# Layer 2: the high part of the turned x is read from its SBUF copy, and one copy alone releases the PSUM bank

## The chip, the cores and the metric

The kernel runs on one core of a Trainium2 chip, in one launch. The metric is the device time of that launch in microseconds (us); lower is better. Engines: PE (TensorE, matmuls and transposes, results in PSUM), ACT (ScalarE), DVE (VectorE), POOL (GpSimd, which works on SBUF alone here) and SP (SyncE, which issues transfers). Each runs its own list in order and waits for the others by semaphores.

## The reference, cut to what matters

Four graph layers on x of 16 batches x 512 nodes x 128 features follow one another: an Euler scheme, a two-layer GCN with batch norms, a masked self-attention and a graph attention. After each: `x = _layernorm(x + layer(x))`. The change lies in the third, "layer 2":

```python
def _L2_gnn_ref(h, W, adj):            # h: (16, 512, 128), W: (128, 384), 4 heads of 32
    qkv = h @ W
    q, k, v = split(qkv)
    mask = jnp.where(adj == 0, -jnp.inf, 0.0)
    scores = jnp.einsum('bhid,bhjd->bhij', q, k) / np.sqrt(HEAD_DIM) + mask
    attn = jax.nn.softmax(scores, axis=-1)
    out = jnp.einsum('bhij,bhjd->bhid', attn, v)
    return out
x = _layernorm(x + _L2_gnn_ref(x, L2_gnn_W, adj), axis=-1)
```

## The kernel before, in words

Layer 2 takes the 16 batches one after another, as a software pipeline. A step s works on several batches at once, each at another stage; each engine has a written list of items with the number of steps by which the item's batch lies behind s (`"x:2"`: the turning of x for batch s-2). The lists are `PE_ORDER`, `ACT_ORDER`, `DVE_ORDER`, `POOL_ORDER` and `SP_ORDER`, repeated for every step (L92 is the loop's end). There is no scheduler: what stands in the list runs in that order, each item after its own waits. Steps count from 0; the first has only the first items, a full step has all.

PE's list for one step, with the items that the prediction uses:

```
v:4 k:3 t2:5 D0:6 D1:6 s0:3 x:2 n:4 t3:5 d:6 T:0 s1:3 o:6 t0:4 V0:5 V1:5 s2:3 q:2 t1:4 V2:5 V3:5 s3:3
```

- T (L1822) turns layer 1's result of batch s; DVE's R (L1732) then adds the residual, into `Xb`.
- x (L1827) turns the normed x of batch s-2 into a PSUM bank. ACT copies it out twice: xc (L1670) as full float32, `xT`, and xh (L1666) cast to fp32r, `xT_hi`. POOL's xl (L1619) subtracts the two, `xT_lo`. The product q takes `xT_hi` and `xT_lo` (L59 to L61).
- s0 to s3 (L1852) are scores of a quarter of the rows, four heads each. DVE's u0 to u3 (L1755) take their masked row maxima.
- t0 to t3 (L1868, then the mask with L1872) are the transposed scores of one head, into the two wide PSUM tiles of 1024 columns. ACT exponentiates each with two activations (E0 to E7, L1693). t0 also needs the first two tiles of u1, whose banks it takes, and POOL adds halves of the exponentials (S0 to S3, L1624) for the denominators.
- V0 to V3 (L1890), D0 and D1 (L1880), d (L1901) and o (L1896) form the output and its denominators and turn them back. DVE's c1 (L1761), c2 (L1768) and r (L1775) divide and add the residual; r alone of these reads two SBUF operands. ACT's y (L174, out `X`) applies the layer norm from step 7 on.

ACT's list: `E0 E1 Y qh E2 E3 f vc kh N E4 E5 e xc nr E6 E7 y xh`. So xc stands before the last two exponentials of the step and xh behind them and behind y. ACT's qh (L1674) waits for the transfers of q and k that SP issued for the batch two before (L1593).

Two PSUM banks, called the ring, serve the short-lived products. One of them holds, in PE's order, v, x, T, o and q (and D). `wait_for_bank` makes PE wait before each of these for the item that emptied the bank; `released` names the semaphore. For the bank that holds x this is `x_hi`, the end of xh. The next user is T; in steps 16 and 17, which have no T any more, it is o. Step 18 has no x in that bank ahead of it.

Of the kernel before, what the change touches and what calls it, by code (L numbers as in the profile page):

```python
# [41 lines left out]
def after(b, per, k=None):  # L42

    return (b + CREDIT) * per + (per if k is None else k)


def hold(eng, gate):


    eng.sem_inc(gate, 1)  # L50


def flat(ap):
    return ap.rearrange("p a b -> p (a b)")
# [44 lines left out]
def tile_of(X, b, t):  # L99
    return X[:, bass.ds(b, 1), t].rearrange("p a d -> p (a d)")  # L100
# [986 lines left out]
def staged(text):  # L1087

    return [(word.split(":")[0], int(word.split(":")[1])) for word in text.split()]
# [374 lines left out]
def layers2_3(nc, m, bank, wide, out):  # L1464
# [4 lines left out]
    with ExitStack() as own:  # L1469
        def sb(name, shape, dt=F32):  # L1470
            return own.enter_context(nc.sbuf_tensor(name, shape, dt))

        def sem(name):
            return own.enter_context(nc.semaphore(name))
# [3 lines left out]
        xT = [sb(f"xT{k}", [P, N]) for k in range(2)]  # L1478
        xTr = [sb(f"xT_{h}", [P, N], F32R) for h in ("hi", "lo")]
# [23 lines left out]
        x_ps = sem("x_turned"); x_hi = sem("xT_high"); x_c = sem("xT_out"); x_lo = sem("xT_low")  # L1503
# [26 lines left out]
        ring = {name: bank[6 + k] for name, k in staged("T:1 x:1 k:0 v:1 q:1 n:0 D0:1 V0:0 d:0 o:1")}  # L1530
# [3 lines left out]

        def released(name, b):

            return {"x": (x_hi, after(b, 1)), "q": (q_lo, after(b, 1)), "k": (k_lo, after(b, 1)),
                    "v": (v_c, after(b, 1)), "n": (n_row, after(b, 1)), "D0": (d_c, after(b, 1)),
                    "V0": (o_c, after(b, 1)), "d": (rcp, after(b, 1)), "o": (o_n, after(b, 1)),
                    "T": (res1, after(b, 1))}[name]  # L1540
# [8 lines left out]
        def run(eng, items, act_on, last=None):  # L1549

            depth = 1 + max(back for _, back in items)

            def step(s, par, alive, nth):
                for name, back in items:
                    if alive[back]:
                        act_on(name, s - back, (par + back) % 2, s, alive)

            pairs(eng, B, depth, step, last=last)
# [13 lines left out]
        @block.sync  # L1572
        def _(sp):
            for h in range(H):
                sp.sem_inc(row_in[h], CREDIT * 16)
                sp.sem_inc(stacked[h], CREDIT * STACKED)

            def transfer(name, b, bp, s, alive):
                h = int(name[2])
                sp.wait_ge(t_ps, after(b - 1, H, h + 1))  # L1580
                hold(sp, gate)
                if name[0] == "d":
                    sp.wait_ge(n_row, after(b, 1))
                    hold(sp, gate)
                    sp.dma_start(q_st[3 * HD:3 * HD + 1, h].bitcast(F32).rearrange("a (t p) -> a t p", p=P),
                                 neg_row[h * NT:h * NT + NT].bitcast(F32)).then_inc(row_in[h], 16)
                else:
                    sp.wait_ge(q_lo, after(b, 1))
                    hold(sp, gate)
                    sp.wait_ge(k_lo, after(b, 1))  # L1590
                    hold(sp, gate)
                    for g, (q, k) in enumerate(((Q_HI, K_HI), (Q_HI, K_LO), (Q_LO, K_HI))):
                        sp.dma_start(qk_st[g * HD:(g + 1) * HD, :, h].bitcast(F32),  # L1593
                                     qkT[bp][h * HD:(h + 1) * HD, q:k + 1:k - q].bitcast(F32)).then_inc(stacked[h], 16)

            run(sp, SP_ORDER, transfer)
            third.sync(sp)
# [41 lines left out]
        @block.scalar  # L1639
        def _(act):  # L1640
            third.act_credits(act)
            for s in (bn, x_hi, x_c, q_hi, k_hi, v_c, n_row, o_c, d_c):
                act.sem_inc(s, CREDIT)
            act.sem_inc(t_exp, CREDIT * EXPS)
            for n in (norm1, norm):
                n.credit_apply(act)

            def projections_free(b):
                for h in range(H):
                    act.wait_ge(stacked[h], after(b - 2, STACKED))  # L1650
                act.wait_ge(s_ps, after(b - 2, TILES))

            def work(name, b, bp, s, alive):
                if name == "N":
                    act.wait_ge(b_ps, after(b - 1, 1))
                    hold(act, gate)
                    act.activation(on[:], m.O[:, bass.ds(b, 1)].rearrange("p a n -> p (a n)"), ACT.Identity,
                                   scale=m.aff2[:, 0, 0:1], bias=m.aff2[:, 1, 0:1]).then_inc(bn, 1)
                elif name == "Y":
                    norm1.apply_act(act, b + CREDIT, bp, Xf[bp], lambda k: Xf[bp][:, k])  # L1660
                elif name == "y":
                    norm.apply_act(act, b + CREDIT, bp, r, lambda k: tile_of(m.X, b, k))
                elif name == "xh":
                    act.wait_ge(x_ps, after(b, 1))
                    act.wait_ge(k_ps, after(b - 1, 1))
                    act.copy(xTr[0][:], ring["x"][:]).then_inc(x_hi, 1)  # L1666
                elif name == "xc":
                    act.wait_ge(x_ps, after(b, 1))
                    act.wait_ge(v_ps, after(b - 2, 1))
                    act.copy(xT[bp][:], ring["x"][:]).then_inc(x_c, 1)  # L1670
                elif name == "qh":
                    projections_free(b)
                    act.wait_ge(q_ps, after(b, 1))
                    act.copy(qkT[bp][:, Q_HI], ring["q"][:]).then_inc(q_hi, 1)  # L1674
                elif name == "kh":
                    projections_free(b)
                    act.wait_ge(k_ps, after(b, 1))
                    act.copy(qkT[bp][:, K_HI], ring["k"][:]).then_inc(k_hi, 1)
                elif name == "vc":
                    act.wait_ge(v_ps, after(b, 1))  # L1680
                    act.wait_ge(av, after(b - 2, NT))
                    act.copy(flat(v[bp][:]), ring["v"][:]).then_inc(v_c, 1)
                elif name[0] == "E":
                    k = int(name[1])
                    h, half = divmod(k, 2)
                    act.wait_ge(t_ps, after(b, H, h + 1))
                    if k == 0:
                        act.wait_ge(av, after(b - 2, NT))
                        act.wait_ge(h_sum, after(b - 2, H))
                    if k == 4:  # L1690
                        act.wait_ge(av, after(b - 1, NT))
                        act.wait_ge(h_sum, after(b - 1, H))
                    act.activation(flat(prob[bp][h][:, 2 * half:2 * half + 2]), wide[half][:], ACT.Exp,  # L1693
                                   scale=SCALE).then_inc(t_exp, 1)
                elif name == "nr":
                    act.wait_ge(n_ps, after(b, 1))
                    for h in range(H):
                        act.wait_ge(row_in[h], after(b - 1, 16))
                    act.activation(neg_row[:], ring["n"][0:TILES, 0:P], ACT.Copy, scale=-1.0).then_inc(n_row, 1)
                elif name == "e":  # L1700
                    act.wait_ge(dn, after(b, 2))
                    act.wait_ge(d_ps, after(b - 1, 1))
                    act.copy(denT[:], ring["D0"][:]).then_inc(d_c, 1)
                elif name == "f":
                    act.wait_ge(av, after(b, NT))
                    act.wait_ge(o_ps, after(b - 1, 1))
                    act.copy(oT[:], ring["V0"][:]).then_inc(o_c, 1)

            run(act, ACT_ORDER, work, last=18)
            item = third.act_items(act)  # L1710
            tail("E0.14 E1.14 E2.14 E3.14 f.13 vc.15 E4.14 E5.14 e.13 nr.15 E6.14 E7.14 3XR.0 3X.0 y.12 E0.15 E1.15 3W0.0 "
                 "E2.15 E3.15 f.14 3W1.0 E4.15 E5.15 e.14 E6.15 E7.15 3G.0 3L0.0 3L1.0 y.13 3XR.1 3L2.0 3L3.0 3X.1 f.15 e.15 "
                 "3E0.0 3W0.1 3W1.1 y.14 3E1.0 3XR.2 3G.1 3L0.1 3L1.1 3X.2 3L2.1 y.15", ACT_ORDER, work, item)
            pairs(act, B, 4, third.in_order(item, third.act_order), last=B, first=3)
            third.act_last(act, item)
# [232 lines left out]
```

## Time and profile before

| | us |
|---|---|
| median of 3 runs | 1008.46 |
| the runs | 1007.96, 1008.46, 1016.79 |
| the profiled execution's own time | 1007.55 |
| its span | 1005.6 |
| PE busy in the span | 886.4 (88%) |
| DVE busy | 643.3 (64%) |
| ACT busy | 505.2 (50%) |
| POOL busy | 362.7 (36%) |

Layer 2 runs from about 457 us to about 860 us of the span; its last steps overlap with layer 3. "m" below is the start of the mask matmuls of t3 (L1872) in a step: a point that every step from 5 on has, shortly before T. The end of a stretch is the start of s2, behind T, s1, o, t0, V0 and V1. In the step whose m is at 603.82, T is at 608.42 and s2 at 614.92. The mean granted clock of TensorE over the span is 0.956 of full speed.

A row of the timeline reads: start, duration, engine, line, operation, output<-input, count, and in brackets the idle time of the engine before it with what ended it.

### The profile page before, as it was taken

Reading aid. Unit: us, or ns where it says so; the run is one execution under the profiler, and the core shown is the slowest. Engines: PE = TensorE matmul, PEld = TensorE weight load, DVE = VectorE, ACT = ScalarE, POOL = GpSimd, SP = SyncE. Lnnn points to the kernel's source line nnn. Section 1 sums busy time; section 2 is a strip of 40 time slices with the busy share of each in tenths; the row PEclk is TensorE's granted clock in tenths of the full one; section 3 lists DMA queues with packets and bytes.
Section 4 is the critical chain, followed back from the end, with each engine's and each line's share of the span. In section 5 each row is a group of like instructions: output and inputs, shape, how many; then the busy total and the mean of one; then the engine's idle time right before and its main releaser. Section 6 shows DMA issues by size and latency. Waiting matters only on the chain. (4 is left out here: it accounts for less than half of the span.)

```text
span 1005.6 us, 20699 instructions
## 1 busy us (share of the span) xinstructions
PE 886.4 (88%) x6039; PEld 632.9 (63%) x6039; DVE 643.3 (64%) x1960; ACT 505.2 (50%) x903; POOL 362.7 (36%) x417
## 2 busy tenths in 40 slices
PE   6999999999998899795688888777888898899996
PEld 5799999999997878432334444333444344577775
DVE  4755554555455776474866666666666573799997
ACT  4322211212112255574356666666666657888884
POOL 4011021011111020003345666655666547355554
PEclk9999999999999899898789899999999899999999
DMA  8000000000001000000332222233233331011111
GB/s 235 21 11 12 22 12 12 21 10 21 10 0 21 22 0 0 1 0 18 70 73 65 64 64 63 63 72 69 63 67 75 78 82 34 2 32 31 31 31 42
DMA packets 34242, 40.74 MB, mean 41 GB/s; under 512 B 6672, under 2 KB 17552, under 8 KB 34192
## 3 DMA queue, kind: packets, MB, share of 16 engines
q1 hardware_dynamic: 32816, 39.87, 16.6%
q8 instruction: 24, 0.39, 0.2%
q10 hardware_dynamic: 1376, 0.27, 0.1%
q14 instruction: 26, 0.21, 0.1%
HBM read 6.43 MB, written 4.19 MB: 11 GB/s over the span
## 5 line engine op out<-in xcount | busy, mean ns | idle before, releaser
L1693 ACT ACTIVATE prob<-wide 128x1024 f32<-128x1024 f32 x128 | 124.1, 1021 | 102.1 <-PE wide L1872 102.1
L1624 POOL TENSOR_TENSOR half_sum<-prob 128x1024 f32<-128x1024 f32 x64 | 150.1, 2368 | 42.3 <-PE bank L1880 41.2
L431 ACT CAST yT<-wide 128x512 fp32r<-128x512 f32 x48 | 28.1, 589 | 206.2 <-PE wide L827 156.8
L1755 DVE CUSTOM_DVE_ANT_0 junk<-wide,mask_ij 128x512 bf16<-128x512 f32 x128 | 82.8, 684 | 64.1 <-PE bank L1852 63.7
L1868 PE MATMUL wide<-qk_st 128*128 128x512 f32 x256 | 92.1, 473 | 2.8 <-ACT prob L1693 1.3
L1755 DVE CUSTOM_DVE_ANT_0 junk<-bank,mask_ij 128x512 bf16<-128x512 f32 x128 | 83.0, 685 | 0.0
L531 POOL TENSOR_TENSOR Xr<-Xf,Xr 128x512 fp32r<-128x512 f32 x16 | 20.4, 1290 | 168.2 <-ACT Xr L426 168.0
L1439 PEld LDWEIGHTS bank<-Wh,pr 128*128 128x128 f32 x512 | 65.2, 191 | 15.9 <-ACT pr L1292 7.0
L1439 PE MATMUL bank<-Wh,pr 128*128 128x129 f32 x512 | 68.5, 278 | 6.7 <-ACT pr L1292 6.0
L59 PE MATMUL bank<-z,L3T_hi 128*128 128x256 f32 x256 | 73.3, 286 | 0.4 <-DVE zf L646 0.4
L60 PE MATMUL bank<-z,L3T_hi 128*128 128x256 f32 x256 | 73.0, 285 | 0.0
L61 PE MATMUL bank<-z,L3T_lo 128*128 128x256 f32 x256 | 72.9, 285 | 0.0
L1868 PEld LDWEIGHTS wide<-qk_st 128*128 128x128 f32 x256 | 52.6, 218 | 27.4 <-DVE mx L1755 15.2
L153 POOL TENSOR_SCALAR n_rstd<-n_aggr 128x4 f32<-128x4 f32 x31 | 6.6, 212 | 166.7 <-DVE n_aggr L146 161.4
L1890 PE MATMUL bank<-prob,v 128*32 128x512 f32 x512 | 65.3, 630 | 1.2 <-ACT prob L1693 1.2
L623 DVE TENSOR_TENSOR yT<-wide,yT 128x512 fp32r<-128x512 f32 x48 | 33.0, 688 | 35.0 <-ACT yT L431 34.8
L1822 PE MATMUL bank<-ident,on 128*128 128x128 f32 x64 | 11.7, 312 | 47.4 <-ACT xT_hi L1666 39.8
L59 PEld LDWEIGHTS bank<-z,L3T_hi 128*128 128x128 f32 x256 | 49.5, 193 | 1.8 <-issue 0.9
L1732 DVE TENSOR_TENSOR Xb<-bank,X 128x512 f32<-128x512 f32 x16 | 11.1, 691 | 61.1 <-PE bank L1822 58.2
L60 PEld LDWEIGHTS bank<-z,L3T_hi 128*128 128x128 f32 x256 | 49.5, 193 | 0.3
L61 PEld LDWEIGHTS bank<-z,L3T_lo 128*128 128x128 f32 x256 | 49.5, 193 | 0.0
L646 DVE TENSOR_TENSOR zf<-bank,G 128x256 f32<-128x256 f32 x64 | 26.9, 420 | 31.2 <-PE bank L61 29.5
(304 smaller groups left out, 2400.8 us busy)
## 6 DMA issues: line engine op xcount, KB each, us to landing
qk_st<-qkT SPq DMA_DIRECT2D x192, 128.0 KB, 2.4
out_dram<-rc SPq DMA_DIRECT2D x15, 256.0 KB, 2.3
Xf<-X SPq DMA_DIRECT2D x14, 256.0 KB, 2.3
A<-in_adj_dram SPq DMA_DIRECT2D x4, 256.0 KB, 4.7
qk_st<-neg_row SPq DMA_DIRECT2D x64, 2.0 KB
Xf<-in_x_dram SPq DMA_DIRECT2D x2, 256.0 KB, 6.7
mask_q<-mask_ji SPq DMA_DIRECT2D x16, 32.0 KB, 1.8
w<-in_L_gnn_W_dram SPq DMA_DIRECT2D x2, 128.0 KB, 2.3
```

Of the source, the lines that this page charges most:

```text
L59: pe.matmul(out, stat[0], mov[0], start=start, stop=False)
L60: pe.matmul(out, stat[0], mov[1], start=False, stop=False)
L61: return pe.matmul(out, stat[1], mov[0], start=False, stop=stop)
L431: act.copy(yT[bb][i][0][:], psum_y[i][:]).then_inc(y_hi, 1)
L623: dve.tensor_tensor(yT[bb][i][1][:], psum_y[i][:], yT[bb][i][0][:].bitcast(F32), ALU.subtract).then_inc(y_lo, 1)
L646: dve.tensor_tensor(zf[:, t], psum_h[k % 2][:, 0:GB * D], G[1 - par][:, 1 if k < NT else 0, t], ALU.add).then_inc(h_sb, 1)
L1439: last = pe.matmul(out_bank[h][:, t * (D + 2):t * (D + 2) + D + 1], pr[par][:, j, k * P:k * P + P], Wh[par][:, j, 0:D + 1], start=(j == 0) ...
L1624: pool.tensor_tensor(flat(half_sum[h][:]), flat(prob[bp][h][:, 0:2]), flat(prob[bp][h][:, 2:4]), ALU.add).then_inc(h_sum, 1)
L1693: act.activation(flat(prob[bp][h][:, 2 * half:2 * half + 2]), wide[half][:], ACT.Exp, scale=SCALE).then_inc(t_exp, 1)
L1755: dve.tensor_tensor_reduce(out=junk[h % 2][:], in0=ROWS[h][:], in1=m.mask_ij[:, i], scale=1.0, scalar=3.0 * MASKED, op0=ALU.add, op1=ALU.m ...
L1868: pe.matmul(bank[j][:], k_st[:, k, j * P:j * P + P], q_st[:, k], start=True, stop=True)
L1890: last = pe.matmul(ring["V0"][c, :], v[bp][:, k, c], prob[bp][h][:, k], start=(k == 0), stop=(k == NT - 1), skip_group_check=True)
```

## The change

The cast xh no longer reads the PSUM bank but `xT`, the float32 copy that xc has put into SBUF, and so it waits for xc (`x_c`) instead of for PE (`x_ps`). The bank counts as free when xc is done. The semaphore of xh stays as it is for those that read `xT_hi`. No instruction is added, dropped or moved on any engine: the lists are the same, and only the wait of T (steps 2 to 15) and of o (steps 16 and 17) names another semaphore.

```diff
--- before.py
+++ after.py
@@ -1534,7 +1534,7 @@
 
         def released(name, b):
 
-            return {"x": (x_hi, after(b, 1)), "q": (q_lo, after(b, 1)), "k": (k_lo, after(b, 1)),
+            return {"x": (x_c, after(b, 1)), "q": (q_lo, after(b, 1)), "k": (k_lo, after(b, 1)),
                     "v": (v_c, after(b, 1)), "n": (n_row, after(b, 1)), "D0": (d_c, after(b, 1)),
                     "V0": (o_c, after(b, 1)), "d": (rcp, after(b, 1)), "o": (o_n, after(b, 1)),
                     "T": (res1, after(b, 1))}[name]
@@ -1661,9 +1661,9 @@
                 elif name == "y":
                     norm.apply_act(act, b + CREDIT, bp, r, lambda k: tile_of(m.X, b, k))
                 elif name == "xh":
-                    act.wait_ge(x_ps, after(b, 1))
+                    act.wait_ge(x_c, after(b, 1))
                     act.wait_ge(k_ps, after(b - 1, 1))
-                    act.copy(xTr[0][:], ring["x"][:]).then_inc(x_hi, 1)
+                    act.copy(xTr[0][:], xT[bp][:]).then_inc(x_hi, 1)
                 elif name == "xc":
                     act.wait_ge(x_ps, after(b, 1))
                     act.wait_ge(v_ps, after(b - 2, 1))
```

## Rows read from the trace of the kernel before

**Rows 1.** Who waited for the cast xh (L1666), over the whole span.

```profile
  PE bank L1822: 39.8, 14
  PE bank L1896: 4.6, 2
```

**Rows 2.** Timeline of PE in the step with m at 603.82: d and T.

```profile
604.18 0.66 PE L1901 MATMUL bank<-ident,denT 128*128 128x128 f32 x4
608.42 0.65 PE L1822 MATMUL bank<-ident,on 128*128 128x128 f32 x4 [3.59 <-ACT xT_hi L1666]
612.70 0.43 PE L1872 MATMUL wide<-mask_q,identb 32*32 32x512 bf16 x16
```

**Rows 3.** Timeline of ACT in the same step: xc, E6 and E7, y, xh, E0 and E1, qh.

```profile
602.43 0.59 ACT L1670 COPY xT<-bank 128x512 f32<-128x512 f32 x1 [0.82 <-PE bank L1827]
...
604.36 1.94 ACT L1693 ACTIVATE prob<-wide 128x1024 f32<-128x1024 f32 x2 [1.19 <-PE wide L1872]
606.19 1.64 ACT L174 ACTIVATE X<-rb,n_shift,n_rstd 128x128 f32 x4
607.73 0.57 ACT L1666 CAST xT_hi<-bank 128x512 fp32r<-128x512 f32 x1
613.39 1.94 ACT L1693 ACTIVATE prob<-wide 128x1024 f32<-128x1024 f32 x2 [5.10 <-PE wide L1872]
...
616.76 0.57 ACT L1674 CAST qkT<-bank 128x512 fp32r<-128x512 f32 x1
```

**Rows 4.** Stretches from m to s2, steps 5, 6, 7, 9, 15, 16, 17, 18; granted clock behind POOL.

```profile
509.03:519.72 10.69, 7.84 (x61) 2.36 (x60) 5.04 (x21) 5.81 (x9) 7.34 (x6) 0.71 0.51 109
532.58:542.47 9.89, 7.33 (x70) 3.59 (x69) 5.72 (x23) 4.19 (x5) 8.73 (x7) 0.83 0.40 88
555.08:566.74 11.66, 7.88 (x69) 4.02 (x68) 5.77 (x23) 5.43 (x9) 9.04 (x8) 0.71 0.33 72
603.82:614.92 11.10, 7.21 (x69) 3.73 (x68) 5.72 (x23) 5.46 (x9) 8.22 (x6) 0.85 0.34 74
747.21:758.29 11.08, 7.19 (x69) 3.73 (x68) 5.72 (x23) 5.60 (x9) 8.47 (x6) 0.85 0.34 75
770.92:780.70 9.78, 6.77 (x65) 2.66 (x64) 4.22 (x14) 6.40 (x11) 7.65 (x5) 0.83 0.47 101
793.33:804.22 10.89, 7.88 (x66) 3.42 (x65) 4.22 (x14) 5.87 (x9) 8.35 (x5) 0.69 0.46 98
816.83:823.24 6.41, 5.61 (x66) 2.42 (x65) 4.13 (x14) 5.14 (x8) 6.41 (x4) 1.00 0.49 107
```

**Rows 5.** Timeline of DVE in the step with m at 603.82: R, u1's second tile, r.

```profile
609.36 0.69 DVE L1732 TENSOR_TENSOR Xb<-bank,X 128x512 f32<-128x512 f32 x1 [4.81 <-PE bank L1822]
...
610.69 0.69 DVE L1755 CUSTOM_DVE_ANT_0 junk<-wide,mask_ij 128x512 bf16<-128x512 f32 x1
...
618.09 0.69 DVE L1775 TENSOR_TENSOR rb<-rb,X 128x512 f32<-128x512 f32 x1
```

**Rows 6.** Timeline of PE and DVE in step 18: s1, and u1's second tile.

```profile
818.54 0.49 PE L1852 MATMUL wide<-qkT 32*128 32x512 f32 x2 [0.69 <-ACT prob L1693]
...
819.84 0.69 DVE L1755 CUSTOM_DVE_ANT_0 junk<-wide,mask_ij 128x512 bf16<-128x512 f32 x1
```

**Rows 7.** A group of ACT by form: a cast of this size from SBUF, in layer 0 (busy, mean ns).

```profile
L426 ACT CAST Xr<-Xf 128x512 fp32r<-128x512 f32 x14 | 8.0, 620 | 0.0
```

**Rows 8.** Timelines of POOL and DVE: S2 and S3 in step 9; S2 and S3, and r, of step 19.

```profile
609.60 4.70 POOL L1624 TENSOR_TENSOR half_sum<-prob 128x1024 f32<-128x1024 f32 x2
837.60 4.73 POOL L1624 TENSOR_TENSOR half_sum<-prob 128x1024 f32<-128x1024 f32 x2
840.18 2.70 DVE L1775 TENSOR_TENSOR rb<-rb,X 128x512 f32<-128x512 f32 x1 [0.18 <-DVE rb L1768]
```

**Rows 9.** SP's issue of the last transfers that qh waits for; time to landing, 590 to 640 us.

```profile
608.78 1.98 SPq L1593 DMA_DIRECT2D qk_st<-qkT  x3
...
DMA to landing us min/median/max: 2.3/2.4/2.5
```

## The prediction, written before the change was run

> **What bounds the kernel now.** I read three views, in this order. First, who waited for the instruction that the change touches: PE stood idle 39.8 us before T in 14 steps, and 4.6 us before o in two more, until xh ended [rows 1]. That is 44.4 us of real PE idle time on the engine that is busiest. Second, the timeline of one full step, to see whether anything else would have held T: d, the item ahead of it, ends at 604.18 + 0.66 = 604.84, T starts at 608.42 [rows 2]. ACT had finished xc at 602.43 + 0.59 = 603.02, before d was even through. But xh stands behind E6, E7 and y and starts only at 607.73 [rows 3]. The bank is held by ACT's order, not by work on the bank. Third, the stretches from m to the start of s2, step by step [rows 4]: steps that wait take 9.78 to 11.66 us, and step 18, which has no x before it in the bank, takes 6.41. It is a control inside the same trace: nearly the same items (no T, no q behind it), no wait for xh, and the whole of it at the full granted clock, 1.00. The waiting steps show means of 0.69 to 0.85: of its two levels, 1.2 and 2.4 GHz, the clock was at the lower one for a good part of what follows the idle time. The reader should see that the wait costs more than its own length.
>
> **The new length of a full step.** Times are counted from m. T can start when d is through: 604.84 - 603.82 = 1.02. R follows T's start by 609.36 - 608.42 = 0.94, and the second tile of u1 follows R by 610.69 - 609.36 = 1.33 [rows 2, 5]; so that tile starts at 3.29. In step 18 it is 823.24 - 819.84 = 3.40 from there to s2 [rows 4, 6], at full clock. Sum: 6.69. Does s1 come in time for it? s1 takes the banks that E6 reads, and in step 18 it starts 818.54 - 816.83 = 1.71 behind m [rows 4, 6]. T's work ends at about the same time, and u1's first tile is only reached at about 2.7. So PE's idle time shrinks to about a tenth of a microsecond, and DVE's chain T, R, u1 is what sets t0.
>
> **The sum over the steps.** Steps 7 to 15 take 11.66, 11.34, 11.10, 11.18, 11.07, 11.17, 11.09, 11.18 and 11.08 us (the first, the third and the last are in [rows 4]), together 100.9. Nine times 6.69 is 60.2, so 40.7 is gained. Step 6 (9.89, without y) gains 3.2. Step 5 (10.69) has neither d nor y; T then comes early and s1 is what u1 waits for, as in step 18: 10.69 - 6.41 = 4.3. Steps 16 and 17 have no T, o waits in its place: 9.78 - 6.41 = 3.4 and 10.89 - 6.41 = 4.5 [rows 4]. Together 56.1.
>
> The first three waits of the 14 lie in steps 2 to 4 and make 39.8 less nine of 3.59 less two of 2.58 and 2.07, which is 2.8. There xh follows xc almost at once, and DVE, still with other tiles, often is not ready for R. Bounds are 0 and 2.8; I take 1.0.
>
> **What the edit costs.** xh reads SBUF instead of PSUM. Its row has 0.57, a cast of the same size from SBUF has 0.620 [rows 3, 7]: 0.05 more, 16 times. In front of it is nothing new to wait for, since xc is long done. It ends at 608.30 + 0.05, 4.53 behind m. The next on ACT is E0, which starts 0.69 behind t0's mask matmuls [rows 2, 3]; those lie 614.92 - 612.70 = 2.22 ahead of s2, so E0 is due at 6.69 - 2.22 + 0.69 = 5.16. The cover is 0.6 us, where it was 5.1 before. I cost the longer cast at nothing; if this cover is gone, all steps pay what xh is late. The Trainium skill, "VectorE: DVE Perf Modes", section on the TRN2 errata, speaks against the edit: it gives ScalarE 52 cycles more from SBUF than from PSUM, an estimate of 43 ns at its 1.2 GHz, and by that the sum stays the same; the trace's difference of 0.05 agrees.
>
> **What is late next.** POOL does not move, for xl, S2 and S3 hang on xh, which keeps its place against m. S3 ends at 609.60 + 4.70 = 614.30, 10.5 behind m [rows 8]. DVE's r does move: it follows s2 by 618.09 - 614.92 = 3.17 [rows 4, 5], so it comes at 9.86 instead of 14.27, into the time of S3. In the trace this pair met once: r started at 840.18, while POOL's additions ran until 842.33, and took 2.70 us until 842.88 instead of 0.69 [rows 5, 8]. So r will wait for S3 and end at 10.53 + 0.55 = 11.08, 0.53 late; in steps 16 and 17, where it comes at 9.58, 0.81 late. DVE's statistics and u3 stand behind it, and t2 waits for u3. The loss is between nothing and 9 x 0.53 + 2 x 0.81 = 6.4 us; v and t2 have some play of their own, so I take 3.0. The Trainium skill, "SBUF — State Buffer", section "SBUF: two separate sides", has a rule for it: a VectorE instruction with two SBUF inputs and a GpSimd one that reads SBUF exclude each other for a whole instruction. By it r is blocked as reckoned here; were r not held, the sum would be 3.0 better. The trace agrees with the rule, by the 2.70.
>
> **The sum.** 56.1 + 1.0 - 3.0 = 54.1. Against the profiled execution's own 1007.55 that is 953.5. The median of the runs lies 0.9 above it, so I predict 954.
>
> **The rivals.**
> - *Only the waits go, the clock does not come back* (967). The wait is 44.4 us; if other gaps keep the clock at its lower level as now, 44.4 - 3.0 = 41.4 is gained. For it: the clock takes some time to return after an idle stretch. Against it: step 18, with 0.69 idle ahead of s1, shows 1.00 throughout [rows 4, 6]. Chance 0.12.
> - *Another wait takes part of the place* (970 to 990). t0 comes 4.4 us earlier and needs its head's row from SP, E0's cover is 0.6, r runs into S3. Each us lost in every full step costs 11 or so; with 1.5 to 3 lost it is 971 to 988. For it: three margins of a microsecond or less in one step. Against it: step 18 has the same order of n, row and t0 without a wait. Chance 0.16.
> - *The transfers collide, and it gets slower.* The early t0 releases the next batch's first set of transfers while the last set for this one, issued from 608.78 to 610.76 [rows 9], is still moving. qh waits for that set. It started at 616.76, 12.94 behind m [rows 3]; it is wanted about 4.4 earlier, near 8.5, and the set lands at most 2.5 behind its last issue, at 9.4 at the latest. DVE takes ql only behind r, at 11.0, so qh may be some 2 late for nothing. Each further us costs one per step. Break-even with the 4.4 gained is a landing 6 to 7 us late, where 2.3 to 2.5 is measured in all; at 8 us late it would be about 1007.5 + 11 x 1.5 = 1024. Against it: the range of the landing is narrow even where the sets follow closely. Chance 0.03.
> - *Nothing happens* (1007). T also waits for ACT's N and for d's place; if one of these ended at the same time as xh, the wait would keep its length. Against it: d ends 3.6 us earlier, and T starts 0.12 behind xh in the step [rows 2, 3]. Chance 0.03.
>
> **How the numbers follow.** The forecast has 0.66; its own range is 949 to 961, from the bounds of the r term (0 and 6.4), of the first steps (0 and 2.8) and two or three microseconds of drift. The full range, 948 to 973, adds the clock rival and the lower end of the partial one. A change within 1% (about 10 us) is no change for this kernel's measurement. Faster by over 1%: 0.66 + 0.12 + 0.16 = 0.94; within: 0.03; slower: 0.03.
>
> **What would show each step.** In the new trace PE's idle time before T and o until xh is gone, T starts within 0.1 of d's end, and the granted clock is 1.00 from m to s2. That stretch is 6.5 to 7.0 in steps 7 to 15, and the distance from m to m falls from 23.9 ((747.21 - 603.82) / 6, [rows 4]) to about 19.7. xh takes 0.62. r takes 1.1 to 1.3 instead of 0.69 in these steps and POOL's S2 and S3 stay at 4.7. ACT's idle time before E0 is near 0.6. Wrong would be: a wait of PE before t0 or q of over half a microsecond (the row, the transfers or xl), a clock under 0.9 in the stretch, or r as short as now.

## The result, and the profile after

| | before | changed |
|---|---|---|
| median, run in turn on one chip | 1008.21 (1007.51 to 1016.79, 4 runs) | 959.13 (955.08, 958.99, 959.27) |
| profiled execution's own time | 1007.55 | 959.27 |
| its span | 1005.6 | 957.2 |
| mean granted clock | 0.956 | 0.969 |

The ratio is 0.9486 [0.9426, 0.9545]: 49 us faster, where 54 were forecast. A fourth run of the changed kernel, 1242.74 at a mean granted clock of 0.65, was a disturbed one and is left out of the ratio.

First, who waited for xh. This is the answer for its line in the changed kernel: durations (ns, min/median/max), the first and last start, and then who waited (us, times).

```profile
L1666 ACT CAST xT_hi<-xT x16: 601/610/622, 468.3 to 752.9; 128x512 fp32r<-128x512 f32 x16
...
  POOL xT_lo L1619: 45.8, 15
```

The two lines of PE in [rows 1], 39.8 and 4.6 us, are gone. Only POOL's subtraction is left, which needs the value and not the bank. The cast takes 0.61 instead of 0.57.

Now one full step, with m at 591.66, against [rows 2]. The timeline of PE:

```profile
591.66 0.43 PE L1872 MATMUL wide<-mask_q,identb 32*32 32x512 bf16 x16
592.03 0.66 PE L1901 MATMUL bank<-ident,denT 128*128 128x128 f32 x4
592.52 0.60 PE L1822 MATMUL bank<-ident,on 128*128 128x128 f32 x4
593.29 0.50 PE L1852 MATMUL wide<-qkT 32*128 32x512 f32 x2 [0.17 <-ACT prob L1693]
...
594.14 0.66 PE L1896 MATMUL bank<-ident,oT 128*128 128x128 f32 x4 [0.35 <-DVE Xb L1732]
594.56 1.42 PE L1868 MATMUL wide<-qk_st 128*128 128x512 f32 x4
595.90 0.43 PE L1872 MATMUL wide<-mask_q,identb 32*32 32x512 bf16 x16
...
598.12 0.50 PE L1852 MATMUL wide<-qkT 32*128 32x512 f32 x2
```

T (L1822) follows d (L1901) with no idle time. It starts 0.86 behind m, not 4.60. What idle time the timeline shows in the stretch is 0.17 before s1 and 0.35 before o, which waits for R's reading of the bank. R and the second tile of u1 on DVE, against [rows 5]:

```profile
593.40 0.69 DVE L1732 TENSOR_TENSOR Xb<-bank,X 128x512 f32<-128x512 f32 x1 [1.00 <-PE bank L1822]
...
594.73 0.69 DVE L1755 CUSTOM_DVE_ANT_0 junk<-wide,mask_ij 128x512 bf16<-128x512 f32 x1
```

The tile ends at 595.42, and the weight load of t0's last matmul, which has waited 0.4 for DVE's row maxima, comes at 595.5. From the tile's start to s2 it is 3.39.

The timeline of ACT in the same step, against [rows 3]:

```profile
590.27 0.59 ACT L1670 COPY xT<-bank 128x512 f32<-128x512 f32 x1 [0.82 <-PE bank L1827]
...
592.21 1.94 ACT L1693 ACTIVATE prob<-wide 128x1024 f32<-128x1024 f32 x2 [1.19 <-PE wide L1872]
594.04 1.64 ACT L174 ACTIVATE X<-rb,n_shift,n_rstd 128x128 f32 x4
595.58 0.61 ACT L1666 CAST xT_hi<-xT 128x512 fp32r<-128x512 f32 x1
596.60 1.94 ACT L1693 ACTIVATE prob<-wide 128x1024 f32<-128x1024 f32 x2 [0.41 <-PE wide L1872]
...
600.57 0.59 ACT L1674 CAST qkT<-bank 128x512 fp32r<-128x512 f32 x1 [0.51 <-DMA qk_st<-qkT]
```

xh stands 3.92 behind m, as before (607.73 - 603.82 = 3.91): ACT's work has not moved, PE's has. E0 comes 0.41 behind xh, where it came 5.10 behind it. And qh now waits 0.51 for its transfers, where it waited for nothing.

The stretches, for m to s2 of steps 5, 6, 7, 9, 15, 16, 17 and 18, as in [rows 4]. Behind the start and end stand the length, the busy time (and count) of PE, PEld, DVE, ACT and POOL, the granted clock, the DMA share and GB/s:

```profile
513.99:520.40 6.41, 5.20 (x61) 2.00 (x60) 5.13 (x21) 4.11 (x5) 3.34 (x2) 1.00 0.36 77
533.02:539.38 6.36, 5.94 (x69) 2.80 (x68) 5.32 (x23) 4.12 (x5) 5.73 (x4) 1.00 0.33 72
551.99:558.35 6.36, 5.94 (x70) 2.80 (x69) 5.31 (x23) 5.50 (x9) 4.19 (x4) 1.00 0.31 65
591.66:598.12 6.46, 5.94 (x69) 2.80 (x68) 5.32 (x23) 5.50 (x9) 3.78 (x3) 1.00 0.32 69
710.06:716.51 6.45, 5.93 (x69) 2.80 (x69) 5.31 (x23) 5.65 (x9) 4.01 (x3) 1.00 0.29 62
729.54:735.95 6.41, 5.61 (x65) 2.42 (x65) 4.12 (x14) 5.65 (x9) 4.23 (x4) 1.00 0.34 73
749.00:755.41 6.41, 5.60 (x66) 2.42 (x66) 4.14 (x14) 5.65 (x9) 4.26 (x4) 1.00 0.30 65
768.48:774.89 6.41, 5.61 (x65) 2.42 (x65) 4.12 (x14) 5.14 (x8) 6.41 (x4) 1.00 0.49 106
```

All steps now look like step 18, the control, which itself has not changed (6.41). PE's busy time in them falls too, from 7.21 to 5.94 in step 9 for the same matmuls, since the granted clock is 1.00 where it was 0.85.

Then what got worse. The timelines of DVE and POOL in the same step, against [rows 5, 8]:

```profile
597.50 4.73 POOL L1624 TENSOR_TENSOR half_sum<-prob 128x1024 f32<-128x1024 f32 x2
...
601.28 1.50 DVE L1775 TENSOR_TENSOR rb<-rb,X 128x512 f32<-128x512 f32 x1
602.32 0.52 POOL L162 TENSOR_SCALAR n_rstd<-n_aggr 128x4 f32<-128x4 f32 x1
602.71 0.68 DVE L1739 TENSOR_TENSOR qkT<-bank,qkT 128x512 fp32r<-128x512 f32 x1
```

r is issued in the middle of S3 and takes 1.50 instead of 0.69; it ends 602.78 - 602.23 = 0.55 behind POOL's addition. It is no single case. This is r's own line in the changed kernel, over all batches; the median was 686 before:

```profile
L1775 DVE TENSOR_TENSOR rb<-rb,X x16: 687/1452/2681, 542.5 to 818.8; 128x512 f32<-128x512 f32 x16
```

The whole account, from the profiled executions, with two points that both have (m of step 5 and m of step 18):

| | before | changed | difference |
|---|---|---|---|
| up to m of step 5 | 509.03 | 513.99 | +4.96 |
| the 13 stretches m to s2, steps 5 to 17 | 142.12 | 83.93 | -58.2 |
| the 13 stretches s2 to the next m | 165.68 | 170.56 | +4.9 |
| from m of step 18 to the end of the span | 188.8 | 188.7 | 0 |

### The profile page after: what moved, and what is told of

The parts are those of the page before. It is cut to its first block and busy times, and to the rows that moved or that the text cites. A ratio compares the mean times of both kernels' runs of the same rounds, so it can differ in the third digit from the quotient of the medians.

```text
span 957.2 us, 20699 instructions
## 1 busy us (share of the span) xinstructions
PE 878.5 (92%) x6039; PEld 626.5 (65%) x6039; DVE 651.8 (68%) x1960; ACT 506.8 (53%) x903; POOL 366.2 (38%) x417
## 5 line engine op out<-in xcount | busy, mean ns | idle before, releaser
L1868 PE MATMUL wide<-qk_st 128*128 128x512 f32 x256 | 88.1, 440 | 3.8 <-ACT prob L1693 1.7
L59 PE MATMUL bank<-z,L3T_hi 128*128 128x256 f32 x256 | 74.2, 290 | 0.0
L1868 PEld LDWEIGHTS wide<-qk_st 128*128 128x128 f32 x256 | 46.3, 192 | 35.4 <-DVE mx L1755 24.6
L1890 PE MATMUL bank<-prob,v 128*32 128x512 f32 x512 | 61.6, 598 | 1.2 <-ACT prob L1693 1.2
L59 PEld LDWEIGHTS bank<-z,L3T_hi 128*128 128x128 f32 x256 | 50.4, 197 | 1.2 <-issue 0.4
L1852 PEld LDWEIGHTS wide<-qkT 32*128 32x128 f32 x128 | 12.4, 187 | 55.0 <-ACT prob L1693 29.2
L1328 DVE SCALAR_TENSOR_TENSOR pr<-bank,Wh,rl 128x512 f32<-128x512 f32 x64 | 45.0, 741 | 1.2 <-PE bank L1451 1.1
```

What stands on the lines that cost most here:

```text
L59: pe.matmul(out, stat[0], mov[0], start=start, stop=False)
L1328: dve.scalar_tensor_tensor(out=pr[par][:, k], in0=bank[4 + k % 2][:], scalar=Wh[par][:, k, S2_SLOPE:S2_SLOPE + 1], in1=rl[par][:, k], op0= ...
L1868: pe.matmul(bank[j][:], k_st[:, k, j * P:j * P + P], q_st[:, k], start=True, stop=True)
L1890: last = pe.matmul(ring["V0"][c, :], v[bp][:, k, c], prob[bp][h][:, k], start=(k == 0), stop=(k == NT - 1), skip_group_check=True)
```

## The experiments

Nine kernels ran. Ratios are to the kernel before, run in turn on the same chip.

**1. Does the gain come from the early release?** The changed kernel, with the bank released by xh again, which still reads SBUF:

```diff
-            return {"x": (x_c, after(b, 1)),
+            return {"x": (x_hi, after(b, 1)),
```

> The cast xh reads SBUF as in the change, but the bank stays held until xh is done. Theory (the gain is the early release alone, the other source costs nothing): PE waits for xh before T as before, about 39.8 us plus 0.05 per step, and the time is 1007 to 1009. Rival (part of the gain comes from the source, since ACT no longer reads the bank): clearly below 1003.

Measured: 1016.52 (1013.72 to 1017.42, 8 runs), the kernel before beside it 1014.4 (1006.89 to 1017.63), ratio 1.0031 [0.9997, 1.0064]. Who waited for xh:

```profile
L1666 ACT CAST xT_hi<-xT x16: 600/608/619, 468.6 to 803.9; 128x512 fp32r<-128x512 f32 x16
...
  PE bank L1822: 40.5, 14
...
  PE bank L1896: 4.7, 2
```

The wait is back (45.2 us in 16 waits, 44.4 before), and the distance from m of step 5 to m of step 18 is 308.74, where it was 307.80. So the release makes the gain, and what the other source costs in these steps is at most the 0.9 between the two. The absolute time lies above the 1007 to 1009 expected of it. Of the kernel before, run in turn with it, 11 of 17 runs do too (1013.44 to 1017.63, the other six 1006.89 to 1008.44), but here it is all eight; no run shows why. Its profiled execution reaches m of step 5 at 513.73, where the kernel before had 509.03. This raised the second question.

**2. Why did the first steps come 5 us late?** One explanation was that T, now early in steps 2 to 4, leaves PE idle for long behind it and so loses clock. The first kernel is the change again, as a control. The second keeps the late release for batches 0 to 2 only. The third adds spare matmuls (a table, `SPARE`, of matmuls whose result nobody reads) behind T in step 2:

```diff
-            return {"x": (x_c, after(b, 1)),
+            return {"x": (x_hi if isinstance(b, int) and b < 3 else x_c, after(b, 1)),
```

```diff
-            SPARE = {("T", 0): 12, ("T", 1): 5,
+            SPARE = {("T", 0): 12, ("T", 1): 5, ("T", 2): 10,
```

> The changed kernel once more, in several executions. Theory (the first steps of layer 2, where the granted clock fell twice between 470 and 491 us, come out in more than one way from execution to execution): times spread over 955 to 960, low ones with a mean clock near 0.978, high ones near 0.969. Rival (the first steps are always as in the profile): all within 0.5 us of 959.

> The change, but for the first three batches T still waits for xh; from batch 3 on xc alone releases the bank. Theory A (the early T of step 2 leaves one idle stretch of 2.7 us before q, where the kernel before had 0.5 and 1.8 apart, and that makes the clock fall): m of step 5 back near 509 to 510 us, the clock 1.00 from 464 to 488, the time steady at 954 to 955. Theory B (the clock of the first steps is chance, whatever the wait): the same spread as the change, 955 to 960.

> The change with ten more spare matmuls behind T of step 2, about 2.2 us of work in the 2.7 us in which PE waits for xl there. They compute nothing that is used. Theory A (the idle stretch makes the clock fall): the clock stays at 1.00 from 466 to 488, step 5's m comes near 510, the time is steady at 954 to 955.5. Theory B (chance): spread as the change, 955 to 960, or a little worse for the extra matmuls.

| | median | runs | ratio | m of step 5 | from there to m of step 18 |
|---|---|---|---|---|---|
| the change again | 957.07 | 954.24 954.37 954.92 959.21 959.76 960.05 | 0.9444 [0.9405, 0.9483] | 508.67 | 254.77 |
| late release in the first steps | 959.18 | 956.00 956.77 959.11 959.26 959.38 959.57 | 0.9448 [0.9412, 0.9484] | 514.25 | 254.53 |
| more spare matmuls | 956.13 | 954.68 955.55 955.87 956.38 957.76 959.98 | 0.9437 [0.9400, 0.9474] | 509.46 | 254.39 |

The change itself comes out at two values, near 954.5 and near 959.5; the profiled execution above was one of the second kind. Two stretches of the span at the first steps (470 to 478 and 485 to 491 us), columns as above, in the changed kernel's first profile:

```profile
470.00:478.00 8.00, 6.29 (x17) 2.85 (x18) 3.60 (x12) 3.45 (x7) 3.71 (x7) 0.57 0.00 0
...
485.00:491.00 6.00, 5.03 (x18) 3.50 (x18) 5.54 (x17) 1.17 (x2) 2.15 (x5) 0.50 0.00 0
```

and of the same kernel, run again:

```profile
470.00:478.00 8.00, 6.56 (x34) 3.23 (x34) 6.25 (x22) 4.66 (x10) 3.52 (x7) 1.00 0.29 61
...
485.00:491.00 6.00, 3.65 (x25) 2.08 (x23) 5.70 (x18) 3.14 (x6) 1.27 (x1) 0.88 0.00 0
```

One kernel, two executions: 18 matmuls in 6 us at a granted clock of 0.50, or 25 at 0.88. The stretches are the same pieces of time and not quite the same instructions, since the first execution is already late in them. For the same instructions, q of the first batch (L59) and the first s0 (L1852), the timeline of PE has, in the first profile:

```profile
471.71 0.76 PE L59 MATMUL bank<-xT_hi,Wr 128*128 128x512 f32 x1 [2.71 <-POOL xT_lo L1619]
...
476.72 0.79 PE L1852 MATMUL wide<-qkT 32*128 32x512 f32 x2
```

and in the second:

```profile
470.24 0.47 PE L59 MATMUL bank<-xT_hi,Wr 128*128 128x512 f32 x1 [2.29 <-POOL xT_lo L1619]
...
473.33 0.50 PE L1852 MATMUL wide<-qkT 32*128 32x512 f32 x2 [0.35 <-issue]
```

The same work takes 5.01 in one and 3.09 in the other. The explanation fell, since the kernel that keeps the old release in these steps shows the low clock as well (0.79 and 0.53), and the change without it can show the high one. A small part of the difference is there before layer 2 begins: from 400 to 457 us, in layer 1, the clock is 0.93 in the executions that reach step 5 near 509 (before, the change again, more spare matmuls) and 0.88 or 0.89 in those that reach it at 514, and the first T starts at 459.29 in the first profile and at 458.23 in the second. That is 1.06 of the 5.32 by which they differ at step 5; the rest comes in layer 2's first steps. The kernel before spreads too, over 10 us (1006.89 to 1017.63). What decides between the values stays open. With the spare matmuls four of six runs were below 957, with the plain change three of six: that tells nothing. With the late release in the first steps the two low runs are 956.00 and 956.77, where the change has 954.24 to 954.92. That may be the early release in these steps or the spread; two runs do not tell.

**3. Is the loss behind s2 r's wait for POOL, or the wait for transfers?** Three orders of ACT's list. The first takes the change and puts xh ahead of y, so that xl, S2 and S3 come earlier. The second puts xh directly behind xc in the kernel before, with the old source and the old release: the bank then comes free early without the change. The third is the change with xh behind nr. The change itself ran beside them.

```diff
-... xc:2 nr:4 E6:5 E7:5 y:7 xh:2")
+... xc:2 nr:4 E6:5 E7:5 xh:2 y:7")
```

> The change, with xh moved on ACT one place forward, ahead of y (E6 E7 xh y). xh ends 1.64 earlier, so xl, S2 and S3 on POOL do too, and S3 ends near 8.9 behind m. Theory (r is late because POOL's S3 and r, both with SBUF operands, exclude each other, and this delays u3 and t2): r takes 0.69 again, the stretch from s2 to the next m falls from 13.23 to 12.7 or 12.8 in steps 7 to 15 and from 13.05 to 12.6 in steps 16 and 17, 5 us in all, and the time lies 4 to 6 below the change. Rival (that stretch is longer because of ACT's qh, which waits for the transfers now): r is short again but the stretch stays near 13.2 and the time does not move.

```diff
-... xc:2 nr:4 E6:5 E7:5 y:7 xh:2")
+... xc:2 xh:2 nr:4 E6:5 E7:5 y:7")
```

> The kernel before (xh reads PSUM, its end releases the bank), with xh moved on ACT directly behind xc. Theory (ACT's order held the bank, not the copy's source): T starts behind d at m + 1.0 as in the change, the stretch from m to s2 is 6.4 to 6.5, and with S3 ending early the one from s2 to m is 12.7; the time lies 4 to 6 below the change. Rival (nr is 0.5 later, so the row of the first head comes late for t0): PE waits before t0, the stretch is 6.9 or more, and the time is that of the change or above.

```diff
-... xc:2 nr:4 E6:5 E7:5 y:7 xh:2")
+... xc:2 nr:4 xh:2 E6:5 E7:5 y:7")
```

> The change, with xh moved on ACT behind nr, ahead of E6. Theory: nr keeps its place, xh ends before t3 is done, so nothing behind it moves; the bank is free when xc is done; r is not held by S3; 4 to 6 below the change and equal to the variant with xh directly behind xc within 1 us. Rival (xl stands on POOL behind S0 and S1 anyway, so an earlier xh than ahead of y brings nothing): equal to the variant with xh ahead of y.

> The changed kernel, on the chip on which the three variants of ACT's order run, for the comparison with them: 954 to 960.

The kernel before took 1010.18 beside these four. The last three columns are from their profiles: the sums over steps 5 to 17 of the stretches s2 to m (165.68 before), the same of m to s2, and r's median.

| | median (lowest) | ratio | s2 to m | m to s2 | r |
|---|---|---|---|---|---|
| the change | 958.92 (954.22) | 0.9473 [0.9429, 0.9517] | 170.58 | 83.94 | 1.452 |
| the change, xh ahead of y | 949.63 (949.24) | 0.9406 [0.9361, 0.9452] | 166.43 | 84.02 | 0.689 |
| before, xh behind xc | 953.01 (952.46) | 0.9427 [0.9384, 0.9470] | 168.10 | 84.23 | 0.687 |
| the change, xh behind nr | 952.35 (949.83) | 0.9422 [0.9376, 0.9467] | 165.50 | 83.98 | 0.689 |

By median and by lowest time all three beat the change, though the intervals of the ratios overlap. From m of step 5 to m of step 18, where the spread of the first steps does not reach, the profiles have 254.52 for the change, 250.45 with xh ahead of y, 252.33 with the old source and 249.48 with xh behind nr. The lowest times, 949.24 and 949.83, are those of the two that keep the change and move xh, and these two cannot be told apart. The timelines of ACT, POOL and DVE with xh ahead of y, in the step that has s2 at 592.10:

```profile
588.00 0.62 ACT L1666 CAST xT_hi<-xT 128x512 fp32r<-128x512 f32 x1
...
589.94 4.74 POOL L1624 TENSOR_TENSOR half_sum<-prob 128x1024 f32<-128x1024 f32 x2
...
594.54 0.58 ACT L1674 CAST qkT<-bank 128x512 fp32r<-128x512 f32 x1 [0.50 <-DMA qk_st<-qkT]
...
595.27 0.69 DVE L1775 TENSOR_TENSOR rb<-rb,X 128x512 f32<-128x512 f32 x1
```

That step's stretch from s2 to the next m in this kernel, columns as above:

```profile
592.10:604.82 12.72, 12.34 (x112) 6.21 (x109) 10.24 (x33) 9.98 (x17) 9.33 (x13) 1.00 0.42 90
```

S3 now ends at 594.68, and r starts 0.59 behind it and takes 0.69. The stretch is 12.72, where the change has 13.24 and before had 12.71. qh's wait of 0.50 for the transfers is still there, so it is not what the change lost; r was. The same stretch in the change:

```profile
598.12:611.36 13.24, 12.66 (x111) 6.21 (x108) 11.03 (x33) 10.00 (x17) 10.67 (x13) 1.00 0.40 86
```

The old source with xh behind xc shows where that rival begins. There nr, the row from which t0's transfer is made, comes 0.5 later, and the transfers of q and k stand behind it. The waits from 510 to 770 us of the span, in that kernel (total us, times, longest):

```profile
ACT qkT L1674 <- DMA qk_st<-qkT: 18.0, 13, 3.1
...
DVE qkT L1739 <- ACT qkT L1674: 1.6, 3, 0.7
...
PE wide L1868 <- DMA qk_st<-neg_row: 0.2, 1, 0.2
```

and with xh ahead of y:

```profile
ACT qkT L1674 <- DMA qk_st<-qkT: 11.2, 13, 2.6
```

At 18.0 us of waiting instead of 11.2, qh has begun to hold DVE's ql (1.6 us, where it is 0.4 with xh ahead of y), and the stretches s2 to m are 1.7 to 2.6 us longer than in the two orders of the change, though r is free there too. So its expectation came in half: T is free and r is short, but its lowest run is 1.8 below the lowest of the change and not 4 to 6 (the medians, with the spread of the first steps in them, are 5.9 apart), and it does not equal the order with xh behind nr (2.6 apart by the lowest runs). PE's wait before t0, which its rival named, is 0.2 in all. In this kernel T waits for xh in three of the first steps only (2.7 us); so the gain needs no SBUF source, only an order in which the second copy doesn't stand behind E6, E7 and y.

**4. What is the wait worth, and what the clock behind it?** The kernel before, with its wait as it is, but from step 5 on PE fills it with 16 bf16 matmuls into an idle bank:

```diff
+                if name == "T" and (not isinstance(s, int) or s >= 5):
+                    pe.wait_ge(s_mx, after(b - 3, TILES, H))
+                    for _ in range(16):
+                        pe.matmul(bank[4][:], m.identb[:], m.mask_ji[:, 0], start=True, stop=True)
```

> The kernel before, with 16 spare matmuls (3.5 us at the full clock, into a bank that u0 has read out) between d and T from step 5 on. They compute nothing that is used; T waits for xh as before and starts where it did, 4.60 behind m. Theory (the wait costs 44.4 us by itself and about 14 more by the clock that falls behind it): the clock is 1.00 from m to s2, the stretch is 10.2 to 10.3 in steps 7 to 15 instead of 11.1 to 11.7, and the time is 7 to 12 below the kernel before. Rival (the longer t0 and V0 behind T come from other waits, not from the clock): the stretch stays at 11.1 and the time does not move.

Measured: 998.87 (994.40 to 1000.75), before beside it 1010.08, ratio 0.9862 [0.9815, 0.991]. The timeline of PE (lines behind the edit lie 4 further down, L1826 is T) in the step with m at 600.60:

```profile
601.45 3.62 PE L1820 MATMUL bank<-mask_ji,identb 128*128 128x512 bf16 x16
605.21 0.65 PE L1826 MATMUL bank<-ident,on 128*128 128x128 f32 x4
607.30 1.41 PE L1872 MATMUL wide<-qk_st 128*128 128x512 f32 x4
```

The stretch m to s2 of that step:

```profile
600.60:610.86 10.26, 9.53 (x85) 4.32 (x85) 5.31 (x23) 5.46 (x9) 7.63 (x4) 1.00 0.37 80
```

T comes 4.61 behind m, exactly as late as before (4.60). But the clock is 1.00, where it was 0.85, and from T to s2 it takes 5.65 instead of 6.50. Work that nobody uses, in a wait, takes 11.2 us off the median, and its highest run, 1000.75, lies below the lowest of the kernel before, 1007.31. The 13 stretches sum to 132.44, 9.7 less than before: so much did PE's idle time cost there beyond its length, where about 14 had been expected. (In steps 16 and 17 o waits, and nothing is filled in.)

## Why the prediction was right

The forecast case came in, 5 us above its number (954 against 959.13) and within its own range, 949 to 961. Two later sets of runs of the same kernel have medians of 957.07 and 958.92.

- **The stretch.** 6.69 was predicted for steps 7 to 15, 6.36 to 6.54 was measured, and 58.2 in all where the sum had 56.1. The chain was right, T, R, the second tile of u1, t0. Its first term was long by 0.16: T starts at 0.86 and not at 1.02, since groups of matmuls that follow one another overlap. The others, the last of them taken from step 18 with its other mix of items, were long by 0.07 together (R by 0.06, the last by 0.01). PE's idle time was not "about a tenth of a microsecond": 0.17 before s1 and 0.35 before o are 0.52. Left out was that o takes the bank behind T and so waits for R, as it did before (0.30). This wait hardly lengthens the stretch, since t0's last matmul waits for the second tile of u1 all the same. For step 9 the account closes: 11.10 - 6.46 = 4.64, of which T's earlier start makes 4.60 - 0.86 = 3.74, and what lies between T and s2 6.50 - 5.60 = 0.90. In the filled wait the same part takes 5.65, so 0.85 of these 0.90 came with the clock.
- **The clock.** The rival in which it doesn't come back (967) falls: 1.00 in every stretch from m to s2. Step 18, the control within the trace of before, was the right witness.
- **xh.** 0.62 predicted, 0.61 measured. It has nothing to wait for, and E0 stands 0.41 behind it where 0.6 was reckoned: still covered. Releasing late with the new source gave a ratio of 1.0031 [0.9997, 1.0064]. The Trainium skill, "VectorE: DVE Perf Modes", section on the TRN2 errata, has 52 cycles more for ScalarE from SBUF than from PSUM. The 0.04 measured, between medians of 0.570 and 0.610 at one place in ACT's order, agrees with it. The place counts as well: ahead of E6 the cast takes 0.592 from PSUM and 0.602 from SBUF.
- **r.** The mechanism was right and its size too small: 4.9 us were lost, where 3.0 was taken between 0 and 6.4. r ends where it was reckoned, 11.12 behind m (11.08) and 0.55 behind POOL's addition. But the stretch is shorter than predicted, so r comes at 9.62 and not at 9.86, and it takes 1.50 and not 1.1 to 1.3. Over steps 7 to 17 the excess of r over 0.69 adds up to 8.7, not 6.4. The play of v and t2 was about right: 3.4 was taken, and 8.7 less the 5.1 that these steps lost is 3.6. The trace of before also had the pair a second time, which the prediction did not count: r at 858.53 took 0.84 and ended 0.55 behind POOL's addition. With r free of S3, the order that has xh ahead of y gives 4.1 back (254.52 to 250.45 from m of step 5 to m of step 18). The Trainium skill, "SBUF — State Buffer", section "SBUF: two separate sides", has the rule that a VectorE instruction with two SBUF inputs and a GpSimd one that reads SBUF exclude each other for a whole instruction. The runs agree: r takes 1.41 to 1.60 in steps 7 to 17 with S3 ahead of it, and 0.69 to 0.71 in the three orders in which S3 ends earlier.
- **Two errors of 2 us that cancel.** The stretches gave 2.1 more than the sum had (58.2 against 56.1) and r cost 1.9 more (4.9 against 3.0). This is not all luck. S3 ends 10.56 to 10.58 behind m in steps 7 to 17, where it ended 10.46 to 10.49 behind it before, whatever the stretch does, and r ends 0.55 later, so a stretch that is shorter by 0.23 mostly makes r's delay longer by as much. The distance from m to m, predicted at about 19.7, is 19.70 in step 9.
- **The transfers.** The rival said that qh would come to wait, and it does, by 0.51 in the step shown. It costs nothing in the change, since DVE takes ql (L1739) only behind r. The margin is small, as the order with nr half a microsecond later shows.
- **The term that failed: "the first steps", +1.0.** The profiled execution has -4.96 there, and this makes the net miss: without it the parts give 58.2 - 4.9 = 53.3 of gain, against 53.1 in the sum for the same steps. What I left out is that executions of one and the same kernel differ by 5 us before step 5, with a granted clock of 0.50 or 0.88 in the same 6 us. The runs near 954.5 are as much the change as those near 959.5. In the prediction "two or three microseconds of drift" stood for it; the spread of the kernel before, 1007.96 to 1016.79, had been in front of me and is of this size. Neither of the two kernels that were to steady the early clock did so. The term itself can be seen where two executions run alike until layer 2: before and the change again both have the first T at 458.23 and the first s0 at 473.33, and then m of step 5 at 509.03 and 508.67. So 0.4 of the 2.8 of waits in steps 2 to 4 comes back, not 1.0. That execution has a span of 952.2, 53.4 less than before, where the sum had 54.1. Whether a run comes out near it or 5 us above was not in the prediction, and that the median lay within the range is in that part luck.

Against the whole of it, waits and clock: the filled wait shows that of the 42.6 us that the nine steps 7 to 15 give (100.9 - 58.3), 8.3 is clock (100.9 - 92.6) and nine waits of 3.59 are 32.3. The remaining 2.0 is 0.22 a step; 0.15 of that is that T overlaps with d when it does not wait (3.74 - 3.59).

## What to carry to other kernels

When several instructions read a PSUM bank, the one that releases it should be the one that stands first in its engine's order. Look at where the last reader stands in that list, not at how long the copies take: here a cast of 0.57 us held the bank until 5.3 us behind the end of the first copy. An idle time of PE costs its own length and then a slower clock behind it, here a quarter more (0.85 to 0.90 on 3.6); a stage of the same trace that has no such wait shows the full price. After such a gain look at once for pairs of VectorE instructions with two SBUF operands and GpSimd work that have moved onto each other; here a swap in ACT's list took the pair apart again and took off another 5 us (949.24 against 954.22, the lowest runs).

## What the runs showed of the hardware that was not expected

- Matmuls whose result nobody reads can pay: 16 in each wait of T from step 5 on gave a ratio of 0.9862 [0.9815, 0.991]. T came no earlier in the step; the granted clock from m to s2 was 1.00 instead of 0.85.
- The granted clock of the same program differs from execution to execution in stretches where PE is partly idle: 0.57 or 1.00 in one stretch of 8 us, 0.50 or 0.88 in one of 6, though not quite the same instructions stand in them. The times of the change fall mostly into two groups 5 us apart; those of the kernel before spread over 10.
- A VectorE instruction that is held by GpSimd does not show as a wait. It shows as a longer duration (1.50 or 2.70 instead of 0.69), so a list of waits doesn't have it. It seems that a GpSimd instruction can be held in turn: L162 starts beside the late r in each of steps 7 to 15 and takes 0.52 there, where all 32 of it took 0.194 to 0.196 before and 0.192 to 0.198 in the three orders in which r is free.
